# A gated attention and dense layer on one core: stored parts of the attention output, sums of q times k on another engine, and another place for the spectra of q

## The reference, cut to what matters

```
qf, kf = fft(q, axis=2), fft(k, axis=2)
corr = ifft(qf * conj(kf), axis=2).real
w, idx = top_k(corr, 12); w = softmax(w)
out = sum_i w_i * v[min(idx_i + pos, L - 1)]
x = x + tanh(g_xattn) * out
n = layernorm(x)
base = n @ W_base.T + b_base
moe = experts chosen by gates of n (A_w, B_w of rank 16)
x = x + tanh(g_ffn) * (base + moe)
```

## Time and profile before

| what | us |
|---|---|
| median of 3 runs | 3030.74 |
| lowest and highest of them | 3028.44, 3033.55 |
| the profiled execution, its own time | 3031.29 |
| its span | 3029.5 |

### The profile page before, as it was taken

One profiled execution on the slowest core, in us unless ns is written; L12 is line 12 of the kernel. 1 busy time (PEld: TensorE's weight loads), 2 busy tenths in 40 slices (PEclk: granted clock), 3 DMA queues, 4 the chain that ended last, 5 costly groups with the idle time before them and its releaser, 6 DMA issues.

```text
span 3029.5 us, 37059 instructions
## 1 busy us (share of the span) xinstructions
PE 2921.9 (96%) x13184; PEld 1466.0 (48%) x13184; DVE 1606.0 (53%) x2738; ACT 1012.6 (33%) x1672; POOL 1454.0 (48%) x577
## 2 busy tenths in 40 slices
PE   4999999999999999997799999999999999999999
PEld 2445554555545554553644444444444444444444
DVE  3899989999999999998722121121211112111111
ACT  4555556555555545441511121111211112111110
POOL 4788888889888888884031211212112121221210
PEclk8999999999999999999899999999999999999999
DMA  8455544555455554423634132331323313233230
GB/s 201 124 123 126 139 110 118 127 132 125 115 122 125 135 117 102 101 73 111 237 98 111 56 111 75 91 111 55 111 72 94 106 60 111 69 97 99 68 97 28
DMA packets 260355, 324.49 MB, mean 107 GB/s; under 512 B 162911, under 2 KB 163487, under 8 KB 245541
## 3 DMA queue, kind: packets, MB, share of 16 engines
q1 hardware_dynamic: 259922, 323.38, 40.1%
q10 hardware_dynamic: 348, 0.18, 0.0%
HBM read 223.76 MB, written 67.21 MB: 96 GB/s over the span
## 4 chain that ended last, share of the span: by engine, by line
PE 84%; DVE 5%; POOL 3%; issue 2%; DMA 2%; ACT 1%; SPq 1%; ACTq 0%; DVEq 0%; POOLq 0%
PE bank L1097 43%; PE bank L488 7%; PE bank L422 7%; PE bank L454 6%; PE bank L472 5%; PE bank L460 3%; POOL spec_o L869 3%; DVE rows_mem L1256 2%; PE bank L1086 1%; PE bank L1087 1%; PE bank L1088 1%; ACT wt L548 1%; PE bank L435 1%; PE bank L405 1%; PE bank L411 1%
## 5 line engine op out<-in xcount | busy, mean ns | idle before, releaser
L1281 POOL TENSOR_TENSOR rows_mem<-norm,rows_mem 128x2048 f16<-128x2048 f32 x31 | 126.1, 4068 | 1220.7 <-ACT rows_mem L1156 1220.7
L1097 PE MATMUL bank<-w_hi,rows_mem 128*128 128x512 f16 x2048 | 489.3, 379 | 3.8 <-DVE rows_mem L1256 3.8
L1097 PE MATMUL bank<-w_hi,xres_mem 128*128 128x512 f16 x2048 | 489.0, 379 | 3.5 <-DVE rows_mem L1256 3.5
L869 POOL TENSOR_TENSOR spec_o<-spec_o,term 128x1024 f32<-128x1024 f32 x190 | 443.3, 2362 | 40.6 <-DVE term L686 40.6
L1249 DVE TENSOR_TENSOR hwt_lo<-bank,hwt_hi 128x128 f16<-128x128 f32 x32 | 9.3, 292 | 790.4 <-ACT hwt_hi L1175 790.4
L1097 PEld LDWEIGHTS bank<-w_hi,rows_mem 128*128 128x128 f16 x2048 | 200.2, 98 | 251.6 <-DVE rows_mem L1256 13.6
L1097 PEld LDWEIGHTS bank<-w_hi,xres_mem 128*128 128x128 f16 x2048 | 200.2, 98 | 250.6 <-DVE rows_mem L1256 12.7
L488 PE MATMUL bank<-spec_o,table 128*128 128x512 f32 x512 | 249.1, 617 | 19.9 <-POOL spec_o L869 15.8
L1097 PE MATMUL bank<-w_lo,xres_mem 128*128 128x512 f16 x1024 | 262.8, 379 | 0.0
L1097 PE MATMUL bank<-w_lo,rows_mem 128*128 128x512 f16 x1024 | 262.8, 379 | 0.0
L422 PE MATMUL bank<-rows_mem,table 128*128 128x512 f32 x512 | 227.7, 598 | 18.0 <-POOL rows_mem L849 15.7
(11 more groups left out here) (182 smaller groups left out, 4876.3 us busy)
## 6 DMA issues: line engine op xcount, KB each, us to landing
rows_mem<-in_x_dram SPq DMA_DIRECT2D x32, 1024.0 KB, 13.0
norm<-x_scratch SPq DMA_DIRECT2D x32, 1024.0 KB, 5.5
rows_mem<-x_scratch SPq DMA_DIRECT2D x32, 1024.0 KB, 7.0
out_dram<-rows_mem SPq DMA_DIRECT2D x32, 1024.0 KB, 4.4
norm<-in_x_dram SPq DMA_DIRECT2D x28, 1024.0 KB, 10.8
rows_mem<-in_ctx_dram SPq DMA_DIRECT2D x256, 64.0 KB
rows_mem<-in_ctx_dram SPq DMA_DIRECT2D x64, 256.0 KB
xres_mem<-in_x_dram SPq DMA_DIRECT2D x256, 64.0 KB
```

Of the source, the lines that this page charges most:

```text
L869: pool.tensor_tensor(to, to, buffer, sign).then_inc(term_added, 1)
L1097: mm = pe.matmul(dense[o][:, :], nt(par, part)[:, k, :], w[:, k, o * 512:(o + 1) * 512], start=(k == 0 and n == 0), stop=False)
L1281: pool.tensor_tensor(norm_lo, norm[:, :], norm_hi, ALU.subtract).then_inc(norm_lo_made, 1)
```

## The change

- `residual`, `load_res` and the ten-part `store` are gone. ACT copies each output tile, scaled by the gate, into a buffer `kept` (`keep_out`: half 1 before `scale_w(i)`, half 0 after it), and one transfer for each step stores it in `parts`. The transposes of the next step wait for these copies (`out_kept`) where they waited for `sine_added`.
- The dense layer forms the rows x plus output itself: for each tile SP loads x (tiles with an even number in eight transfers of 16 rows, odd ones in one transfer with the rows of each group of 16 reversed) and the cosine part, POOL adds, SP loads the sine part into the same buffer, POOL adds or subtracts, SP stores the rows in the scratch x2 (`form`). This is done for tile i+3 in step i. There is one buffer `row` where there were two, and the store of tile i stands ahead of the load of row i+1, which waits for that store.
- `sum_qk` leaves POOL. DVE makes the second pair of products in PSUM, in place, and adds and subtracts the first pair (`q_times_k` now has six operations).
- `q_spectra(i+1)` stands between the two output tiles of step i.
- Tile 0 is formed in attention step 31 on POOL, and its statistics stand on DVE in that step ahead of `largest(31)`; the normalising follows in step 32 on ACT.

The core of the diff:

```diff
@@ q_times_k
-                    dve.tensor_tensor(prod_b[:, 0:2, :], imag, k[:, 3:5, :], ALU.mult)
-                    dve.tensor_tensor(prod_a[:, 2:4, :], imag, k[:, 0:3:2, :], ALU.mult).then_inc(q_used, 1)
+                    dve.tensor_tensor(real, imag, k[:, 3:5, :], ALU.mult).then_inc(qk_made, 1)
+                    dve.tensor_tensor(imag, imag, k[:, 0:3:2, :], ALU.mult).then_inc(qk_made, 1)
+                    dve.wait_ge(qk_made, 4 * i + 3)
+                    dve.tensor_tensor(prod_a[:, 0:2, :], real, prod_a[:, 0:2, :], ALU.add).then_inc(q_used, 1)
+                    dve.wait_ge(qk_made, 4 * i + 4)
+                    dve.tensor_tensor(prod_a[:, 2:4, :], imag, prod_b[:, 2:4, :], ALU.subtract).then_inc(q_used, 1)
@@ scalar_attention
+                def keep_out(c, four, h):
+                    if h == 1 and least(c) >= 1:
+                        act.wait_ge(parts_stored, 16 * c)
+                    act.wait_ge(out_made, 2 * c + 2 - h)
+                    act.activation(kept[:, h, :, :], pair(four, 1 - h), ACT.Copy, scale=gates[:, 0:1]).then_inc(out_kept, 1)
@@ vector_attention, step
+                    if most(i) == STEPS - 1:
+                        statistics(dve, 0)
                     if most(i) == STEPS:
                         late_sums(i - 1)
-                        statistics(dve, 0)
                         weights_lo(dve, 0, 2)
@@ sync_dense
                 def step(i, par):
                     if fmost(i) + 1 < ROWS:
                         turn(i + 1, 1 - par)
-                    if fmost(i) + 2 < ROWS:
-                        load_norm(i + 2)
+                    if fmost(i) + 3 < ROWS:
+                        form(i + 3, 1 - par)
+                    sp.wait_ge(out_ready, 4 * (i + 1))
...
+                        sp.dma_start(out_half[i // 2, 0, :, ::-1, :], row).then_inc(out_stored[1], 16)
                     if fmost(i) + 1 < ROWS:
                         load(i + 1, 1 - par)
-                    sp.wait_ge(out_ready, 4 * (i + 1))
-                    sp.dma_start(out_rows[i], row[:, par, :]).then_inc(out_stored[par], 16)
-                load_norm(1)
+                form(1, 1)
                 load(0, 0)
+                form(2, 0)
@@ gpsimd_dense
+                def form(i, par):
+                    pool.wait_ge(norm_loaded[par], (144 * (i // 2), 32 * (i // 2 + 1))[par])
+                    pool.tensor_tensor(norm[:, :], norm[:, :], addend, ALU.add).then_inc(formed, 1)
+                    pool.wait_ge(sine_loaded, 16 * i)
+                    pool.tensor_tensor(norm[:, :], norm[:, :], addend, (ALU.add, ALU.subtract)[par]).then_inc(formed, 1)
```

More of the change, by code:

```diff
@@ L496, in tensor_attention @@
                 v_spectra(0, 0, X(0))
+                q_spectra(0, X(0))
                 pe.wait_ge(ident_loaded, 16)
@@ L515, in step @@
                             turn_weights(pe, 0)
+                    if most(i) + 1 < STEPS:
+                        q_spectra(i + 1, other)
+                    if least(i) >= 1:
                         out_tiles(i - 1, (phase - 1) % NCH, mine, 0)
@@ L973, in flamingo_kernel @@
             GATE_OPS, LN2_OPS = 11, 9
-            FLOOP = (2, ROWS - 2)
+            FLOOP = (2, ROWS - 4)
             def fleast(i):
@@ L1127, in tensor_dense, with deviation_rows, normalise_rows @@
                 tiles(pe, step)
+            def deviation_rows(act, i):
+                act.wait_ge(ln2_step, LN2_OPS * i + 3)
+                act.activation(std_ln2[:, :], var_ln2[:, :], ACT.Sqrt).then_inc(ln2_sqrt, 1)
+            def normalise_rows(act, i):
+                act.wait_ge(ln2_step, LN2_OPS * (i + 1))
+                act.wait_ge(x2_kept, 16 * (i + 1))
+                act.activation(norm[:, :], norm[:, :], ACT.Identity, bias=ln2_bias[:, :],
+                               scale=ln2_scale[:, :]).then_inc(normed, 1)
             def scalar_dense(act):
@@ L1255, in finish @@
                         dve.wait_ge(dense_made, 4 * i + o + 1)
-                        dve.scalar_tensor_tensor(out=row[:, par, cols], in0=dense[o][:, :], scalar=out_gate[:, :],
-                                                 in1=row[:, par, cols], op0=ALU.mult, op1=ALU.add).then_inc(out_ready, 1)
+                        dve.scalar_tensor_tensor(out=row[:, cols], in0=dense[o][:, :], scalar=out_gate[:, :],
+                                                 in1=row[:, cols], op0=ALU.mult, op1=ALU.add).then_inc(out_ready, 1)
                 def step(i, par):
```

209 lines of the change are left out of this document (103 added, 106 removed).

## The result

| what | us |
|---|---|
| changed kernel, median of 4 runs | 3284.49 (3284.31 to 3286.26) |
| kernel before, median of 4 runs beside it | 3029.59 (3026.61 to 3033.55) |
| ratio | 1.084, 95% interval 1.082 to 1.086 |
| span of the profiled execution | 3282.5, clock 0.958 |

The account below looks back on a forecast made before the run. PE's summed instructions were taken to bound the kernel. The terms, 2.5 - 8 - 0.5 + 20.5 = +14.5 us on the profiled 3031.3, gave 3045.8, forecast as 3045 us, range 3031 to 3080.

Parts of the forecast that it names:

- Steady attention, +2.5: Steady attention steps: output tile 0's copy delays the second pair of transposes, 0.05 to 0.1 us for each of 30 steps.
- rival 4: Moved q spectra and sums do nothing for time, steps 0 to 2 included: 3053 us; counted inside the forecast case's 0.60.
- Steps 0 to 2, -8: First attention steps: moved sums, no residual loads and fewer POOL sums bring step 2's transposes to 127 us from 134.96.
- Hand-over, one store for ten transfers, -7.8: Attention to dense layer: step 31's single store and no residual on DVE bring weight refills forward, -7.8 us.
- Hand-over, the block, +7.3: Step 31: tile 0's small DVE statistics wait for POOL's sums, `largest(31)` starts 10.6 us later, 3.3 given back: +7.3.
- Start of the dense layer, a wait of 18.4: PE waits 18.4 us for tile 1's transposes after `base(0)`; with 2.1 for low clock, +20.5 us.
- The loop, 45.3 and so 0: Dense loop on SP takes 45.3 us a tile, fits PE's 47.47 by 2.2, costs 0; upper bound 49.3.
- Rival 1: The dense loop doesn't fit: at 48.7 us, 30 tiles lose 1.2 each less 4 of lead, 3078 us; chance 0.18.

Follow-up runs that it names:

- sums_pool: The changed kernel with the two sums of q times k back on POOL instead of DVE: 3422.04 us, ratio 1.129 to the kernel before.
- q_back: The changed kernel with `q_spectra` back at the start of its own step: 3337.32 us, ratio 1.101 to the kernel before.
- stat_late: The changed kernel with tile 0's statistics back behind the late sums, not ahead of the last search: 3273.74 us, ratio 1.080 to the kernel before.
- all-plain kernel: The changed kernel with x loaded and output stored as plain blocks of 128 rows in all dense tiles, leaving out the reference's row order: 3043.04 us.

## Why the prediction was wrong, step by step

- **Steady attention, +2.5**: +0.6 between the transposes of step 1 and those of step 31 (1233.7 us against 1233.1). The wait of 0.34 us at the second pair of transposes came as worked out (0.35), and the gap of 0.24 us went. What it left out is told under rival 4.
- **Steps 0 to 2, -8**: the transposes begin at 128.08, forecast 127, against 134.96. -6.9 in this pair of traces; in thirteen other runs with all three parts they begin between 125.3 and 128.9. The split was off: the prediction gave the moved sums 2.5 by themselves and the rest to the residual's loads, POOL's two sums and `q_spectra` together. In sums_pool, which lacks only the moved sums, the transposes begin at 136.28, so that nothing of the gain is left; in q_back, which lacks only the move, at 127.85, so that nothing is lost.
- **Hand-over, one store for ten transfers, -7.8**: -8.5, by stat_late's 126.3 us from step 31's transposes to the first logits against 134.9. About right; no run has the residual removed and the ten transfers kept, so the two aren't parted.
- **Hand-over, the block, +7.3**: the mechanism right, the size 8.8 by the same two points (135.1 against 126.3), and 10.8 by the medians of the whole kernel. DVE's search begins 10.1 us later than without it (1392.95 against 1381.45, less the 1.4 by which this execution was already behind); 10.6 was forecast. 6.3 of these 10.1 are waits for POOL, the rest is the statistics' own time. Only 1.3 us come back behind it, where the prediction gave back 3.3. With the others the first logits came 6.0 us early (-6.9 + 0.6 + 0.3), and the sum, -8 - 0.5 + 2.5, also gave 6.0: that they agree so closely is luck, since the three terms are off by 1.1, 0.8 and -1.9.
- **Start of the dense layer, a wait of 18.4**: 32.4. In the all-plain kernel PE waited 18.4: its transposes landed 65.5 us after the first load, forecast 66.6, and PE was ready for them after 47.1, forecast 48.2. So the chain was right, and the form of the transfers was what it had mis-sized.
- **The loop, 45.3 and so 0**: this is the step that failed. Two of its terms, "x and cosine part 7.2 or 8.7" and "x2 and output row landing 7.2", were priced from the earlier trace rows, loads of 128 whole rows, though the diff shows another form for each of them. Measured, 16.3 and 12.7 for the first, 11.1 and 9.3 for the second; 7.56 us over PE's 47.47 for each of 30 tiles, 227 of the 253 us. With plain transfers the sum was right to 1.4 us and the forecast of 3045 to 2 (3043.04). The upper bound of 49.3 was drawn from the same rows, so it could not hold the unknown either; and by the prediction's own count even 49.3 means 30 tiles at 1.8 us less the lead of 4, so 3096, which lies outside its range. No row of before shows a megabyte in 8 x 16 reversed form alone. Its bound had to come from the side where half of the engines work, and this is an estimate: twice the 4.7 of the earlier trace rows for x, and 4.7 for the share of the cosine part on the same engines. That gives 14.1, and a loop over 47.47.
- **Rival 1** (the loop doesn't fit) was the case that came, at 3284 and not at 3078. It had 0.18, on a margin of 2.2 us out of nine terms, two of them with transfers in a form that the trace had not shown.
- **Rival 4** said that without the moved spectra and sums all would be 8 us slower. They are worth 53 and 138 us in the changed kernel (3337.32 and 3422.04 without them). The steady step came out right because all its parts were there; the prediction never asked what each covers.

## What to carry to other kernels

Price a transfer by a row of the same form: split, order and outer count, not by its bytes; where none exists, bound it by the engines that its outer count leaves, here half. When work is taken off a tight loop and prepared two or three tiles ahead, write down for each engine in order what of tile i stands behind what of tile i+3, since a single order put right only renames the wait. A reordering belongs to the work that it was made for: the same move of `q_spectra` costs 153 us in one kernel and saves 53 in the other. And a short wait of PE in every step can cost more than its length, by the lower clock behind it.

## What the runs showed of the hardware

- Eight blocks of 16 rows in one transfer keep half of the DMA engines busy, in either order of rows: a share of 0.49 alone, and 147 GB/s beside another load, against 261 with sixteen blocks of 8 rows.
- Two transposing transfers beside a store of that form took 14.0 us to issue instead of 7.6, and 5.7 beside a store in eight parts.
- A DVE operation of 0.16 us with two SBUF inputs takes up to 2.3 us beside POOL's sums, once for each such operation: 6.3 us in a chain of statistics whose new place cost the whole kernel 10.8 us.
- Waits of PE of 2.8 us in each step, with up to 1.4 more behind them, took the granted clock of an attention stretch from 1.00 to 0.95, one of 3.0 us to 0.97, and the products behind them took longer (5.33 us for 3.78, 8.86 for 7.17). Behind waits of 1.9 us they didn't (3.63 us).
